# Dense experts against routed ones: every token's row scattered to its two experts, and the attention of eight batches in one stream

## The reference

```python
x = x + attention(layernorm(x))          # per batch: q = xn Wq (16 heads of 192), kv = xn Wkv_a (64 + 64),
                                         # layernorm of the 64 latents, scores, softmax, values, Wout
# x = x + moe(layernorm(x)):
logits = x @ gate_w                      # 2048 tokens, 8 experts
scores = softmax(logits)
topk_w, topk_idx = top_k(scores, 2)      # two experts for a token, weights not renormalised
g = silu(einsum('td,edh->teh', x, w_gate)) * einsum('td,edh->teh', x, w_up)    # h = 176
routed = einsum('teh,ehd,te->td', g, w_down, comb)    # comb is 0 but for the two experts
shared = silu(x @ sw_gate) * (x @ sw_up) @ sw_down    # hidden size 352
out = routed + shared
```

## Time and profile before

| | us |
|---|---|
| median of three runs (784.86, 800.9, 806.77) | 800.9 |
| the profiled execution, its own time | 781.86 |
| its span in the trace | 780.1 |

### The profile page before, as it was taken

The page is one execution under the profiler, slowest core; times in us unless marked ns, Lnnn a source line. Parts: engine busy times, 40 slices in busy tenths (PEclk is TensorE's granted clock), DMA queues, the critical chain, the costliest instruction groups (busy, mean ns, idle before and its releaser), DMA issues.

```text
span 780.1 us, 17956 instructions
## 1 busy us (share of the span) xinstructions
PE 733.0 (94%) x5924; PEld 708.6 (91%) x5924; DVE 543.7 (70%) x1269; ACT 437.5 (56%) x1158; POOL 508.9 (65%) x587
## 2 busy tenths in 40 slices
PE   7969999999899999999999998999999998999997
PEld 7759889999899999998899998999999998999997
DVE  6679878597647975498745976379754987369543
ACT  3669754586418842297416863198523974169421
POOL 5438558684768846686566847688465955679244
PEclk9999999999999998999999999999999999999999
DMA  8940000000000000000000000000000000000000
GB/s 239 285 137 2 2 14 1 29 2 3 13 2 27 0 13 0 0 27 0 13 0 27 0 4 10 0 27 0 13 0 7 20 0 13 0 15 1 1 1 14
DMA packets 20226, 18.76 MB, mean 24 GB/s; under 512 B 2816, under 2 KB 19680, under 8 KB 20192
## 3 DMA queue, kind: packets, MB, share of 16 engines
q1 hardware_dynamic: 19360, 18.13, 7.6%
q10 hardware_dynamic: 832, 0.21, 0.1%
HBM read 16.23 MB, written 2.10 MB: 23 GB/s over the span
## 4 chain that ended last, share of the span: by engine, by line
PE 39%; POOL 25%; issue 20%; DVE 7%; ACT 3%; POOLq 1%; DVEq 0%; ACTq 0%
PE ps_q L245 19%; POOL probs L1394 11%; PE ps_y L245 10%; POOL qswap L1384 6%; POOL qf L1389 5%; PE ps_s L245 3%; PE ps_o L245 2%; PE ps_t L1001 1%; PE ps_t L926 1%; ACT qswap L1084 1%; DVE q_lo L305 1%; DVE qf L1212 1%; PE ps_o L887 1%; PE ps_t L1041 1%; DVE score L1270 1%
## 5 line engine op out<-in xcount | busy, mean ns | idle before, releaser
L1394 POOL TENSOR_TENSOR probs<-probs,rinv 128x512 f32<-128x512 f32 x128 | 131.5, 1040 | 56.3 <-DVE rinv L1225 56.3
L1166 ACT ACTIVATE probs<-ps_q 128x256 f32<-128x256 f32 (+1 forms) x112 | 42.9, 383 | 159.3 <-PE ps_q L245 158.6
L400 POOL TENSOR_TENSOR pT_hi<-probs,one 128x256 fp32r<-128x256 f32 x112 | 75.2, 672 | 82.9 <-DVE probs L1320 61.8
L1110 ACT ACTIVATE probs<-ps_s,nmax 128x256 f32<-128x256 f32 x256 | 119.1, 476 | 14.6 <-DVE nmax L1221 13.6
L1317 DVE TENSOR_TENSOR probs<-ps_q,probs 128x256 f32<-128x256 f32 x88 | 37.3, 424 | 102.7 <-ACT probs L1166 96.1
L1389 POOL TENSOR_TENSOR qf<-qf,qswap 128x512 f32<-128x512 f32 x63 | 91.8, 1458 | 17.5 <-DVE qf L1212 9.2
L1084 ACT ACTIVATE qswap<-ps_q 32x512 f32<-32x512 f32 x128 | 75.5, 590 | 44.0 <-PE ps_q L245 42.4
L305 DVE TENSOR_TENSOR pT_lo<-ps_t,pT_hi 128x512 fp32r<-128x512 f32 x128 | 86.8, 678 | 13.5 <-ACT pT_hi L1084 13.4
L1221 DVE TENSOR_REDUCE nmax<-ps_s 128x2 f32<-128x512 f32 x128 | 87.3, 683 | 10.3 <-PE ps_s L245 8.3
L1384 POOL TENSOR_TENSOR qswap<-qswap,qsin 128x512 f32<-128x512 f32 x63 | 81.1, 1287 | 18.5 <-ACT qswap L1084 18.5
L245 PE MATMUL ps_s<-kT_hi,q_hi 128*128 128x256 f32 x256 | 78.8, 308 | 12.4 <-DVE q_lo L305 8.8
(11 more groups left out here) (208 smaller groups left out, 2512.0 us busy)
## 6 DMA issues: line engine op xcount, KB each, us to landing
wq_raw<-Wq_dram SPq DMA_DIRECT2D x16, 192.0 KB, 4.3
xnext<-x_dram SPq DMA_DIRECT2D x8, 256.0 KB, 2.8
wout_raw<-Wout_dram SPq DMA_DIRECT2D x8, 256.0 KB, 4.8
xin<-x_dram SPq DMA_DIRECT2D x8, 256.0 KB, 2.7
out_dram<-x SPq DMA_DIRECT2D x8, 256.0 KB, 2.2
mg_raw<-w_gate_dram SPq DMA_DIRECT2D x4, 352.0 KB, 6.5
mu_raw<-w_up_dram SPq DMA_DIRECT2D x4, 352.0 KB, 6.6
md_raw<-w_down_dram SPq DMA_DIRECT2D x3, 384.0 KB, 6.0
```

The lines of the kernel that those rows point to most:

```text
L400: return gp.tensor_tensor(hi, src, ones.to_broadcast(list(src.shape)), ALU.mult)
L1110: last = nc.scalar.activation(probs[h % 3][:, j, :], L.ps_s[h % 2][:, j, :], ACT.Exp, bias=nmax[:, h, j:j + 1], accum_out=rsum[:, h, j:j + 1])
L1166: nc.scalar.activation(gate[m % 2][0:rows, :], L.ps_q[m % 2][0:rows, 0, :], ACT.Silu).then_inc(ev.silu_done.sem, 1)
L1394: gp.tensor_tensor(probs[h % 3][:, :, :], probs[h % 3][:, :, :], rinv[:, h, :].unsqueeze(2).to_broadcast([P, NT, S]), ALU.mult).then_inc(e ...
```

## The change

The expert stage of each batch is taken out, and with it the dense chunks and the combine table. In its place:

- **One stream** of 65 rounds for the 64 head pairs of all batches, written out without loops; the order inside a round is the old one. Preparation of the next batch and residual, layernorm, turned rows, logits and routing of the previous one are placed in fixed rounds (r is the round in the batch): r0 `rank` and `places` of the batch two back, r0 and r1 `prep_x`, r2 `prep_kv` and `residual`, r3 `prep_kn` and `normal_f`, r4 and r5 `turned_lo`, r5 moments, r6 `prep_k`, normalised rows and `gate_max`, r7 `masks`. Probabilities are turned into `ps_t[0]` alone: the other buffer is `misc`, for the work added to the rounds. Splits of the expert weights lie at ends of rounds.
- **Routing to places**: `masks` marks first and second choice, `rank` (five matmuls with triangular and all-one matrices) counts, and `places` makes a row number for each token and choice. POOL sends the normalised rows to a DRAM buffer, sorted by expert, with four indirect DMAs of 128 rows for a batch (`scatter`); eight more write zeros behind the last row of each expert (`clear`).
- After the stream the shared expert of batches 0 to 2 lies between the last projections and batch 7's routing. Then **39 tiles** of 128 rows of one expert each. SP reads a tile's first row number and loads it (`load_rows`, four buffers), PE turns it, reads the tile's expert number and multiplies with dynamically addressed weights (`rows_gate_up`, 6 matmuls of 352 columns; `rows_down`, 6 of 256), and SP stores the result (`store_rows`).
- Last, POOL gathers each token's two results with 32 indirect DMAs (`gather`, three buffers of a batch) while PE computes the shared expert of batches 3 to 7; DVE adds weight times row (`finish`) and SP stores.

```diff
+ROOM = B * S + P
+TILES = TOP * B * S // P + E - 1
+ROWS = E * ROOM + E * P
+FIRST = 3
...
+            def load_rows(j):
+                if j >= 4:
+                    sp.wait_ge(ev.xt_full, j - 3)
+                row = nc.sync.value_load(row0_i[0:1, j:j + 1], min_val=0, max_val=ROWS - P)
+                sp.dma_start(xg[j % 4][:, :], xs[bass.ds(row, P), :]).then_inc(ev.xg_loaded[j % 4], 16)
+
+            def store_rows(j):
+                sp.wait_ge(ev.y_done, j + 1)
+                sp.dma_start(ys[tile(j), :], yb[j % 3][:, :]).then_inc(ev.y_stored[j % 3], 16)
...
+            for j in range(TILES):
+                if j + 5 < TILES:
+                    load_rows(j + 5)
+                store_rows(j)
...
-            def turn(i, h):
-                pe.wait_ge(ev.pn_done.sem, ev.pn_done.upto(i, h + 1))
-                if h < 2:
-                    pe.wait_ge(ev.cb_done.sem, ev.cb_done.before(i, ER))
-                else:
-                    pe.wait_ge(ev.plo_done.sem, ev.plo_done.upto(i, h - 1))
...
+            def turn(h):
+                pe.wait_ge(ev.pn_done, h + 1)
+                if h >= 1:
+                    pe.wait_ge(ev.plo_done, h)
                 for c in range(NT):
                     for j in range(NT):
-                        last = nc.tensor.transpose(L.ps_t[h % 2][:, c, tile(j)], probs[h % 3][:, j, tile(c)], L.ident[:, :])
-                last.then_inc(ev.t_full.sem, 1)
-
-            def attend(i, h):
...
+            def rank(b):
+                pe.wait_ge(ev.masks_done, b + 1)
+
+                for n, (terms, at) in enumerate((([(L.before, 0)], 0), ([(L.ones, 0), (L.before, 1)], 1), ([(L.ones, 0), (L.ones, 1)], 2))):
+                    for m, (stat, j) in enumerate(terms):
+                        last = nc.tensor.matmul(L.misc[:, at * E:(at + 1) * E], stat[:, :], both[:, j, :], start=m == 0, stop=m == len(terms) - 1)
+                last.then_inc(ev.rank_full, 1)
...
+            def rows_gate_up(j):
+                experts[j] = nc.tensor.value_load(expert_i[0:1, j:j + 1], min_val=0, max_val=E - 1)
+                pe.wait_ge(ev.xtlo_done, j + 1)
+                if j == 0:
+                    pe.wait_ge(ev.part_lo, splits_upto(L, PARTS - 1))
+                if j >= 2:
+                    pe.wait_ge(ev.u_done, j - 1)
+                mgu = [[t[:, k, bass.ds(experts[j], 1), :, :].rearrange("p e g h -> p (e g h)") for t in (L.mgu_hi, L.mgu_lo)] for k in range(KD)]
+                last = three(flat2(ps_g[j % 2])[:, 0:2 * H], [(xt_hi[j % 3][:, k, :], xt_lo[j % 3][:, k, :], *mgu[k]) for k in range(KD)])
+                last.then_inc(ev.g_full, 1)
...
+            def rows_down(j):
+                pe.wait_ge(ev.utlo_done, j + 1)
+                if j == 0:
+                    pe.wait_ge(ev.part_lo, splits_upto(L, PARTS + DOWNS - 1))
+                if j >= 2:
+                    pe.wait_ge(ev.y_done, j - 1)
+                md = [[t[:, c, bass.ds(experts[j], 1), :].rearrange("p e m -> p (e m)") for t in (L.md_hi, L.md_lo)] for c in range(HC)]
+                three(L.ps_s[j % 2][:, 0, :], [(ut_hi[j % 2][0:HK, c, :], ut_lo[j % 2][0:HK, c, :], *md[c]) for c in range(HC)]
+                      ).then_inc(ev.y_full, 1)
...
+            for g in range(PAIRS + 1):
+                i, r = divmod(g, NP)
+                if pair(g + 4):
+                    query(g + 4)
+                if r == 0 and batch(i - 2):
+                    rank(i - 2)
+                if r == 6 and batch(i + 1):
+                    prep_k(i + 1)
+                if pair(g - 1):
+                    turn(2 * (g - 1) + 1)
+                if pair(g + 1):
+                    scores(2 * (g + 1))
+                if pair(g - 3):
+                    project(g - 3)
+                if pair(g + 1):
+                    scores(2 * (g + 1) + 1)
...
+                if r in (4, 5) and batch(i - 1):
+                    turn_f(i - 1, r - 4)
+                if r == 6 and batch(i - 1):
+                    logits(i - 1)
+                if pair(g - 1):
+                    attend(2 * (g - 1))
+                if pair(g):
+                    turn(2 * g)
+                if pair(g - 1):
+                    attend(2 * (g - 1) + 1)
...
+            for j in range(TILES + 2):
+                if j < TILES:
+                    rows_gate_up(j)
+                if 0 <= j - 1 < TILES:
+                    units_turn(j - 1)
+                if j + 2 < TILES:
+                    rows_turn(j + 2)
+                if 0 <= j - 2 < TILES:
+                    rows_down(j - 2)
...
+            for g in range(PAIRS + 1):
+                i, r = divmod(g, NP)
+                if g >= 1 and pair(g + 1):
+                    query_lo(g + 1)
+                if pair(g + 3):
+                    query_cos(g + 3)
+                if pair(g):
+                    inverse(2 * g)
+                if pair(g - 1):
+                    probs_lo(2 * (g - 1))
+                if pair(g - 2):
+                    attended_lo(g - 2)
+                if pair(g):
+                    inverse(2 * g + 1)
+                if r == 6 and batch(i + 1):
+                    prep_k(i + 1)
+                if r == 7 and batch(i - 1):
+                    masks(i - 1)
+                if pair(g + 1):
+                    maxima(2 * (g + 1))
+                if pair(g - 1):
+                    probs_lo(2 * (g - 1) + 1)
...
+                if r == 0 and batch(i - 2):
+                    places(i - 2)
+                if r in (0, 1) and batch(i + 1):
+                    prep_x(i + 1, r)
+                if r == 2 and batch(i + 1):
+                    prep_kv(i + 1)
+                if r == 2 and batch(i - 1):
+                    residual(i - 1)
+                if r == 3 and batch(i + 1):
+                    prep_kn(i + 1)
+                if r == 3 and batch(i - 1):
+                    normal_f(i - 1)
+                if r in (4, 5) and batch(i - 1):
+                    turned_lo(i - 1, r - 4)
+                if r == 5 and batch(i + 2):
+                    prep_moments(i + 2)
+                if r == 6 and batch(i + 2):
+                    prep_normal(i + 2)
+                if r == 6 and batch(i - 1):
+                    gate_max(i - 1)
+                if g in part_round:
+                    split_lo(part_round[g])
+                if g in down_round:
+                    split_lo(down_round[g])
...
+            def scatter(b):
+                pool.wait_ge(ev.slots_done, b + 1)
+                pool.wait_ge(ev.xhf_done, b + 1)
+                for k in range(TOP):
+                    for j in range(NT):
+                        gp.indirect_dma_start(xs[:, :], bass.IndirectOffsetOnAxis(L.slots[:, b, k, j:j + 1], 0), xhat_f[:, j, :], None
+                                              ).then_inc(ev.scattered, 16)
...
+            def clear():
+                pool.wait_ge(ev.ends_done, 1)
+                for e in range(E):
+                    gp.indirect_dma_start(xs[:, :], bass.IndirectOffsetOnAxis(L.ends[:, e:e + 1], 0), L.zero_rows[:, :], None
+                                          ).then_inc(ev.cleared, 16)
...
+            def gather(b):
+                if b >= 3:
+                    pool.wait_ge(ev.fin_done, b - 2)
+                for k in range(TOP):
+                    for j in range(NT):
+                        gp.indirect_dma_start(got[b % 3][:, k, j, :], None, ys[:, :], bass.IndirectOffsetOnAxis(back[:, b, k, j:j + 1], 0)
+                                              ).then_inc(ev.gathered[b % 3], 16)
...
+                normal(2 * g)
+                if r == 1 and batch(i - 2):
+                    scatter(i - 2)
+                normal(2 * g + 1)
...
+            scatter(B - 2)
+            power(var_f, rstd_f, ev.varf_done, ev.rsf_done, B - 1)
+            scatter(B - 1)
+            clear()
+            for n in range(3):
+                pool.wait_ge(ev.y_stored[n], 16 * len(range(n, TILES, 3)))
+            pool.wait_ge(ev.back_done, 1)
+            for b in range(B):
+                gather(b)
```

1601 lines of the change are left out of this document (848 added, 753 removed).

## The result

| us | before | the change |
|---|---|---|
| median of five runs | 786.36 | 864.51 |
| lowest to highest | 779.94 to 806.77 | 857.69 to 876.0 |
| ratio, with its 95% interval | | 1.097 (1.087 to 1.107) |
| profiled execution, span | 781.86, 780.1 | 876.0, 874.2 |

The forecast was 768, the range 690 to 835. The chip's runs lie above all of it.

A forecast was written before the change was run, and what follows sets the result against it. The prediction took PE's array work (94% busy) to bound the kernel, with DVE nearly full in attention. Setup 55, stream 503, routing end 54, tiles 106, tail 48 and 2 outside the span gave 768 us; range 690 to 835.

The forecast's parts named there:

- The ring: Attention rounds: DVE's subtractions, PE's turn and scores, and DVE's maxima wait on each other; 5.85 us a round, 374 for 64.
- Rival A: Stream: the ring does not close, DVE's work alone counts, 427 us and not 503; total 692, chance 0.17.
- the extras: DVE's routing, preparation, moments, normalisation and residual work placed in the rounds lengthens the ring by its own time; 104 us.
- the splits: Thirteen splits of expert weights at ends of rounds, about 1.0 us each; 13 us.
- Rival E: Stream not unbroken: routing has in-order waits on every engine, 0.4 us a round, 26 more; total 794, chance 0.11.
- X: POOL's time for one indirect DMA in scatter, clear and gather, taken as 1.2 us.
- rival C: Scatter, clear and gather: each indirect DMA costs POOL its landing; at X = 2.2, total 836; chance 0.14.
- From the last round to the first tile: Batch 7's routing chain of 34 us, then scatter and clear, their landing and the first load; 54 us.
- tiles: 39 expert tiles at 2.6 us each, limited by PE's 2.44 and SP's queue, plus 5 to fill and drain; 106 us.
- rival D: Tiles with half their time waiting may fall to the lower PE clock, 57 us more; total 825, chance 0.09.
- The tail: Last store, 32 gathers with PE's shared expert under them, a landing, last finish and store; 48 us.
- Before the stream: Setup block up to the first matmuls of query 4, taken as hardly changed; 55 us.

The follow-up runs named there:

- b1: The kernel before, with turn(h) waiting for the probs_lo of head h-1 instead of h-2; 848.0 us, ratio to before 1.083.
- k2: The change, with two spare DVE reductions ahead of the first maxima of each round; 860.1 us.
- e1: The change, with DVE's part of the 13 weight splits in the stream one round later than ACT's part; 832.0 us.
- e7: The change, with DVE's places, moments, normalised rows, turned rows and splits before the first maxima, the last two one round later; 789.1 us, ratio to before 1.005.
- e8: The change, with SP writing zeros over the whole buffer in the first rounds instead of eight clearing indirect DMAs; 853.4 us.
- e10: e7 joined with e8, 66 spare transposes, eight gather buffers (two batches under way) and every finish behind the last shared expert; 769.8 us, ratio to before 0.983.
- f1: The change, with 90 instead of 40 spare transposes on PE at its start; 854.1 us.
- e4: The change, with eight gather buffers instead of three, so no gather waits for finish; 891.5 us.
- f2: e12 with 40 instead of 66 spare transposes at the start; 805.0 us over ten runs.
- e12: e10, with key/value preparation, residual, normalised keys and rows, first turned half moved ahead of the next round's first maxima; 754.5 us, ratio to before 0.964.

## Why the prediction was wrong

**The ring was there.** "turn(h) now waits for probs_lo of head h-1" and its price of 5.5 to 5.98 a round hold: a plain round took 5.72, forecast 5.85, and b1 shows the wait by itself to cost 64 us (848, above the 830 to 840 that were expected) where rounds could be 4.95. Rival A, that it does not close, is refuted.

**The step that failed** is the sentence that what is put between the maxima and the next `q_lo`, "or before the maxima, lengthens this ring by itself, by DVE's time": 104 for the extras and 13 for the splits. With plain rounds at 5.72, all that is more than a plain round cost 567 - 366 = 201 us, where the sum had 129 with the bursts of scatters. Two things are wrong in it.
- The place decides. Ahead of the first maxima DVE waits for scores (84 us over the stream), and k2 put 126 reductions there, 79.5 us busy, for 8.7 us. What I priced alike in both places costs little or nothing in one and its full time in the other, as long as nothing waits there.
- Behind the maxima an extra costs its own time and the wait in front of it. The change puts DVE's half of a split or of turned rows in the same round as ACT's half, behind everything else of ACT. Compare rounds of one kind: r1 with a split took 10.66 (batch 3), without one 7.00 (batch 6), so 3.66 and not 1.0; e1, which parts the two halves, brings the first to 6.99. The sum had no term for such a wait: before, these halves mostly stood in the expert stage, where DVE was half idle.

With the extras moved (e7) a round takes 7.93, near the 7.86 of the sum, but there DVE's idle time hides work that the sum had not hidden: two errors that cancel. Rival E named in-order waits in the stream, though those of the routing, and priced them at 26 us; the waits of the splits alone were 30 (e1), and what order costs in all was 57 (540.2 less 483.7). Its 0.4 us a round was not worked out from a row. It could have been: the chain from ACT's copy to DVE's subtraction, and where ACT stands in its own list when DVE asks, are both in the order of the change.

**Small terms of the stream.** The extras of a batch as they are listed add up to 14.8 and not to 15.5, some 5 us too much in the 104, and in the other direction from the miss. The sentence that 127 and about 90 of the 199 us come back does not close either: it gives more than was removed, under a sum that forecasts a gain of 14. The bursts of four scatters were put at 2 us each; round r1 of batch 7 has one and took 5.72, so they are covered. Masks were put at 3.2 and took 5.2 (280.23 to 285.39) in round 23 but 2.4 (667.20 to 669.58) after the stream. The score rows of both, with POOL's beside the first:

```profile
280.41 2.30 DVE L1376 TENSOR_SCALAR score<-eprob,einv 128x8 f32<-128x8 f32 x2
...
283.02 1.03 DVE L1382 COPY first<-sentinel 128x14 f32<-128x14 f32 x1
...
667.39 0.37 DVE L1376 TENSOR_SCALAR score<-eprob,einv 128x8 f32<-128x8 f32 x2
```

```profile
280.39 1.04 POOL L1618 TENSOR_TENSOR probs<-probs,rinv 128x512 f32<-128x512 f32 x1 [0.96 <-DVE rinv L1339]
281.39 1.29 POOL L1611 TENSOR_TENSOR qswap<-qswap,qsin 128x512 f32<-128x512 f32 x1
282.76 1.26 POOL L1614 TENSOR_TENSOR qf<-qf,qswap 128x512 f32<-128x512 f32 x1
```

Two instructions on 8 columns took 2.30 us beside a busy POOL and 0.37 beside an idle one, and they end with POOL's: the scores at 282.71 where `qswap` ends at 282.68, the copy of 14 columns at 284.05 where `qf` ends at 284.02. By "SBUF — State Buffer" of the Trainium skill, section "SBUF: two separate sides", VectorE, in some modes or with two SBUF inputs, and GpSimd share a port pair that whoever starts first holds for its whole instruction; these rows agree. The trace of before has 0.75 or 1.17 for the same two, in the stage where POOL has more room, and my sum took the price from the 0.75.

**The indirect DMA was right.** X was taken at 1.2; the starts of gathers in one batch stand 1.25 to 1.48 apart:

```profile
802.17 1.09 POOL L1640 DMA_INDIRECT got<-routed_out,back  x1 [110.07 <-DMA routed_out<-yb]
803.57 1.09 POOL L1640 DMA_INDIRECT got<-routed_out,back  x1 [0.30 <-issue]
804.97 0.95 POOL L1640 DMA_INDIRECT got<-routed_out,back  x1 [0.30 <-issue]
```

So rival C, a landing for each, is refuted: in e7, with the same loop, gathers land 2.9 us after their issue in the median, and the next is issued long before. "DMA: Bandwidth & Descriptors" of the Trainium skill, section "Anatomy of one DMA — SWDGE (gpsimd) path", has most of a fixed 2.0 us in the receipt of the write; the trace agrees with it so far as issues do not wait for the landing.

**From the last round to the first tile** 54 us were forecast and measured, and its parts hold too: batch 7's first scatter starts 34 us behind the rounds, as forecast, and from there to the first load it is 17.8 against 17.0. The **tiles** take 2.50 us each (first products of DVE from 701.41 to 796.38, 38 steps) against 2.6. Their clock:

```profile
700.00:797.00 97.00, 90.47 (x606) 81.42 (x604) 39.88 (x114) 47.97 (x151) 0.00 (x0) 0.99 0.32 102
```

0.99, so rival D, a clock that falls in the tiles, is refuted. It fell elsewhere.

**The tail**, 48 in the sum, is the second error: "32·X = 38.4 of gathers" took them as one unbroken row. With three buffers a gather waits for `finish` three batches back, which stands on DVE behind a shared expert that has to be computed first:

```profile
831.27 0.95 POOL L1640 DMA_INDIRECT got<-routed_out,back  x1 [8.80 <-DVE x L1480]
...
841.77 0.94 POOL L1640 DMA_INDIRECT got<-routed_out,back  x1 [5.80 <-DVE x L1480]
```

Four such waits (8.80, 5.80, 5.68, 5.57) are 25.9 us in this trace. Not all of it is the ring: in e8, with the same tail and no halt of PE, the waits are 5.34, 5.80 and 5.63, 16.8 in all, and the tail is 63.3. So about 18 of the 27 us missed are the ring, and the other 9 go with PE's halt and its lower clock in the profiled execution. Naming what is queued behind a wait that the change adds would have found it: the ring is written out in `gather` and in DVE's list. In e10 the same work without that ring takes 51.4, against 48 less 2.6 in the sum.

**Before the stream**, 55 was "hardly changes"; it was 75.6 in the profiled run. In e1, which has its clock back from 26 us on, the first maxima start at 59.82 and not at 75.11, so 15 of the 20 us are the clock. The block computes what it did, at half the clock. It is a cost of this execution: in three of the ten traces with 40 spare transposes and the change's weight block the clock came back early, and why is open.

In one line: of the 108 us, 64 are the stream, of which 30 are waits in front of splits (e1) and most of the rest is the place of DVE's other extras (e7); 27 are the tail, some 18 of them the ring of the gathers; 20 are the block before the stream, 15 of them its clock.

## What to carry to other kernels

When work is moved from a stage with slack into a software-pipelined round, price a place in the queue and not a duration: find the engine's idle stretch in the round, and ask for each moved instruction whether its operand is ready when the queue comes to it. Halves of a pair that two engines compute one after the other belong in different rounds. Where buffers are fewer than batches, draw the ring from the wait to the engine that ends it before calling a row of transfers unbroken.

## What the runs showed of the hardware

- In the change PE was granted 0.50 for some 50 us from 12 us on, in which it was 100% busy; in e1, with the same code and a longer pause before, the clock was back at 27 us, and with the pause filled (f1) it did not fall in the first 40 us. Busy is not enough to bring the clock back there.
- Indirect DMAs of 128 rows of 1 KB cost POOL 1.25 to 1.5 us each whatever lands when. While they were issued without a pause PE stood still for 27 us (e4) and 21 us (f2) inside a product, and for 3 us in the change; in e12, e7 and e8 it did not, at the same pace of issue.
- DVE instructions on 8 and 14 columns that took 0.2 us beside an idle POOL took 1 us and more beside a busy one, and ended within 0.03 us of POOL's.
- 18.9 MB of zeros written under the first rounds (e8) cost no time that these runs can show.
